# A conditional residual block: the first batch's three small products in plain fp32, and a reordered prologue

## The reference

```
x = x + gamma * layernorm(x + relu(x @ W1 + b1) @ W2 + b2) + beta     (adapter, 256 -> 64 -> 256, language index)
x = x + (x @ Ws^T + bs)                                              (256 -> 256, subject index)
x = x + gated sum of 2 expert nets and 3 shared nets, each relu(x @ wi) @ wo, 256 -> 1024 -> 256
x = x + masked softmax pooling of x                                  (scores from tanh(x @ W + b) @ v)
```

## Time and profile before

| what | value |
|---|---|
| median of 3 runs | 519.26 us (519.24 to 519.38) |
| the profiled execution's own time | 519.18 us |
| its span, first to last instruction | 517.4 us |
| PE busy | 508.7 us (98%) in 2455 instructions |
| DVE, ACT, POOL busy | 325.1 (63%), 262.7 (51%), 232.6 (45%) us |
| mean granted TensorE clock | 0.999 of full speed |
| HBM read, written | 46.76 MB, 2.10 MB |

### The profile page before, as it was taken

How to read it: one execution, slowest core, us unless ns; L and a number is a source line. 1 busy time by engine, 2 the same in 40 slices (tenths; PEclk the granted TensorE clock), 3 DMA queues, 4 the chain that set the end, 5 groups by cost and what they waited for, 6 DMA issues and landing times.

```text
span 517.4 us, 7007 instructions
## 1 busy us (share of the span) xinstructions
PE 508.7 (98%) x2455; PEld 419.4 (81%) x2455; DVE 325.1 (63%) x603; ACT 262.7 (51%) x500; POOL 232.6 (45%) x199
## 2 busy tenths in 40 slices
PE   7899999999999999999999999999999999999997
PEld 4688888888888788888888788888888878888984
DVE  7688223884566864776558675488456686444377
ACT  4655454544447573544446655454444756444233
POOL 2654445445354454444544445444535445655021
PEclk9999999999999999999999999999999999999999
DMA  5634333222224322322223533422222222240002
GB/s 177 191 117 133 103 118 126 82 82 82 82 82 132 103 81 82 122 82 82 81 84 91 147 138 103 121 83 81 82 82 82 81 82 82 94 140 12 0 1 81
DMA packets 44554, 49.30 MB, mean 95 GB/s; under 512 B 7396, under 2 KB 34280, under 8 KB 44520
## 3 DMA queue, kind: packets, MB, share of 16 engines
q1 hardware_dynamic: 42904, 47.03, 28.2%
q10 hardware_dynamic: 1616, 1.84, 1.1%
HBM read 46.76 MB, written 2.10 MB: 94 GB/s over the span
## 4 chain that ended last, share of the span: by engine, by line
PE 96%; DVE 1%; ACT 1%; ACTq 1%; POOL 0%; issue 0%; DVEq 0%
PE ps_hid L789 14%; PE ps_hid L794 14%; PE ps_hid L790 14%; PE ps_net L846 13%; PE ps_net L847 13%; PE ps_net L851 13%; PE ps_net L818 2%; PE ps_side L551 1%; PE ps_side L475 1%; PE ps_side L479 1%; PE ps_side L474 1%; PE ps_side L485 1%; PE ps_side L488 1%; PE ps_side L659 1%; PE ps_side L527 1%; ACTq L1085 0%
## 5 line engine op out<-in xcount | busy, mean ns | idle before, releaser
L1730 DVE SCALAR_TENSOR_TENSOR hid_lo<-ps_hid,hid_hi 128x512 fp32r<-128x512 f32 x160 | 110.5, 690 | 162.7 <-ACT hid_hi L1053 161.7
L1813 POOL TENSOR_TENSOR wi_lo<-raw_wi,wi_hi 128x512 fp32r<-128x512 f32 x78 | 104.2, 1336 | 223.8 <-ACT wo_hi L1032 121.0
L1053 ACT ACTIVATE hid_hi<-ps_hid 128x512 fp32r<-128x512 f32 x160 | 95.6, 598 | 206.0 <-PE ps_hid L794 205.3
L789 PE MATMUL ps_hid<-x2T_hi,wi_lo 128*128 128x512 f32 (+1 forms) x332 | 125.6, 381 | 0.0
L790 PE MATMUL ps_hid<-x2T_hi,wi_hi 128*128 128x512 f32 (+1 forms) x332 | 125.2, 379 | 0.0
L846 PE MATMUL ps_net<-hid_hi,wo_hi 128*128 128x512 f32 x304 | 120.7, 397 | 0.0
L847 PE MATMUL ps_net<-hid_hi,wo_lo 128*128 128x512 f32 x304 | 118.6, 390 | 0.0
L1814 POOL TENSOR_TENSOR wo_lo<-raw_wo,wo_hi 128x512 fp32r<-128x512 f32 x78 | 101.6, 1302 | 0.0
L794 PE MATMUL ps_hid<-x2T_lo,wi_hi 128*128 128x512 f32 (+1 forms) x332 | 99.0, 379 | 0.0
L851 PE MATMUL ps_net<-hid_lo,wo_hi 128*128 128x512 f32 x304 | 93.7, 389 | 0.0
L790 PEld LDWEIGHTS ps_hid<-x2T_hi,wi_hi 128*128 128x128 f32 x332 | 62.4, 188 | 11.9
(11 more groups left out here) (321 smaller groups left out, 506.4 us busy)
## 6 DMA issues: line engine op xcount, KB each, us to landing
raw_wi<-in_L_cond_share_wi_dram SPq DMA_DIRECT2D x23, 512.0 KB, 3.7
raw_wo<-in_L_cond_share_wo_dram SPq DMA_DIRECT2D x23, 512.0 KB, 4.8
raw_wi<-in_L_cond_expert_wi_dram SPq DMA_DIRECT2D x16, 512.0 KB, 3.7
raw_wo<-in_L_cond_expert_wo_dram SPq DMA_DIRECT2D x16, 512.0 KB, 4.8
x_rows<-in_x_dram SPq DMA_DIRECT2D x3, 512.0 KB, 5.8
out_dram<-out_rows SPq DMA_DIRECT2D x5, 256.0 KB, 5.4
gate_w<-in_L_cond_gate_w_dram SPq DMA_DIRECT2D x1, 1024.0 KB, 5.3
subj_w<-in_L_cond_weight_dram SPq DMA_DIRECT2D x3, 256.0 KB, 2.7
```

What stands on the lines that cost most here:

```text
L789: mm(dst, wi_lo[:, w, k, c], x2T_hi[:, k, rows], start=(k == 0), stop=False)
L1053: fn(hid_hi[:, ring(b, q)], ps_hid[:, ring(b, q)], ACT.Relu).then_inc(hid_hi_ready, 1)
L1730: v.scalar_tensor_tensor(out=hid_lo[:, ring(b, q)], in0=ps_hid[:, ring(b, q)], scalar=0.0, in1=f32(hid_hi[:, ring(b, q)]), op0=ALU.max, op ...
L1813: g.tensor_tensor(wi_lo[:, w], raw_wi[:, half % 2, :, c], f32(wi_hi[:, w]), ALU.subtract)
```

## The change

For batch 0 alone, the adapter's two products and the subject product are made in fp32 from unsplit operands. x transposed is kept in x1T (not opT_hi), the bias row b2 becomes row 64 of w2b against a row of ones in hT, and each of the four row tiles has its own bank (`adapted_bank`). x is added on TensorE, by a product with the identity, for tiles 0 and 2, and by VectorE for tiles 1 and 3; statistics are taken tile by tile. ScalarE runs a one-column copy, and with it the table load, right behind the x loads. SP issues b1 ahead of w1 and b2 ahead of w2. ScalarE's order becomes hid0, x_beta(0), x_beta(1) (behind a wait for beta), hid1, norm0, wi of pair 0, subj_wT, wo of pair 0, norm1. TensorE interleaves: hidden(0), tiles 0 and 1, hidden(1), tiles 2 and 3, subj_w, transposes of half 0, 3 fillers, the subject product's first block of half 0, transposes of half 1, its second block, then half 1. The other fillers behind the first 7 go. The step names are adapted, and stage A of the later batches is untouched but for writing hT[0:A].

```diff
-    WARM_XT, WARM_ADAPT, WARM_SUBJ, WARM_NORM, WARM_HALF = 7, 2, 2, 5, 5
+    WARM_XT, WARM_SUBJ = 7, 3
...
-        w2 = sb("w2", [A, D])
-        b2 = sb("b2", [ONE_HI + 1, D])
+        w2b = sb("w2b", [ONE_HI + 1, D])
+        w2, b2 = w2b[0:A], w2b
...
-        hT = sb("hT", [A, S])
+        hT = sb("hT", [A + 1, S])
...
         out_rows = sb("out_rows", [P, R, D])
+        first_subj_wT = out_rows[:, 0:KD]
...
+        def adapted_bank(r):
+            return (ps_net[:, 0], ps_net[:, 1], ps_hid[:, 0], ps_hid[:, 1])[r][:, 0:D]
...
                 with nc.allow_non_contiguous_dma(reason="a few vectors, one element to a partition"):
+                    sp.dma_start(b1[:], L0_b1[la].rearrange("o a -> a o")).then_inc(b1_in, 16)
                     sp.dma_start(w1[:], L0_W1[la].rearrange("o (k p) a -> p (o k) a", p=P)).then_inc(w1_in, 16)
-                    sp.dma_start(b1[:], L0_b1[la].rearrange("o a -> a o")).then_inc(b1_in, 16)
+                    sp.dma_start(b2[ONE_HI:ONE_HI + 1], L0_b2[la]).then_inc(b2_in, 16)
                     sp.dma_start(w2[:], L0_W2[la].rearrange("o a d -> (o a) d")).then_inc(w2_in, 16)
-                    sp.dma_start(b2[ONE_HI:ONE_HI + 1], L0_b2[la]).then_inc(b2_in, 16)
...
                 for h in range(2):
-                    rows = rows_half(h)
-                    pe.wait_ge(p_act.sem, p_act.at(0, f"xhi{h}"))
-                    pe.wait_ge(p_pool.sem, p_pool.at(0, "w1_lo"))
-                    w1_hi, w1_lo = side_by_side(w1_st)
-                    product(ps_hid[0:A, h, 0:HS], [(w1_hi[:, k], w1_lo[:, k], opT_hi[:, k, rows], opT_lo[:, k, rows]) for k in range(KD)],
-                            (p_dve.sem, p_dve.at(0, f"xlo{h}"))).then_inc(p_pe.sem, 1)
-                keep_warm(WARM_ADAPT, warm)
-                for h in range(2):
-                    pe.wait_ge(p_pool.sem, p_pool.at(0, "w2_lo"))
-                    pe.wait_ge(p_dve.sem, p_dve.at(0, f"hlo{h}"))
-                    pe.wait_ge(p_act.sem, p_act.at(0, f"hup{h}"))
-                    adapt_half(ps_net[:, h], h).then_inc(p_pe.sem, 1)
-                keep_warm(WARM_SUBJ, warm)
+                    adapter_hidden(h)
+                    for r in (2 * h, 2 * h + 1):
+                        adapted_rows(r)
                 pe.wait_ge(subj_in, 16)
                 transpose_subj(ps_net[:, 2], True).then_inc(p_pe.sem, 1)
-                keep_warm(WARM_NORM, warm)
-                for h in range(2):
-                    if h == 1:
-                        keep_warm(WARM_HALF, warm)
-                    pe.wait_ge(p_act.sem, p_act.at(0, f"xb{h}"))
-                    pe.wait_ge(p_dve.sem, p_dve.at(0, f"norm{h}"))
-                    pe.wait_ge(p_act.sem, p_act.at(0, f"norm{h}"))
-                    transpose_half(ps_side[:, h], norm, h).then_inc(p_pe.sem, 1)
-                pe.wait_ge(p_dve.sem, p_dve.at(0, "subj_w_lo"))
-                for h in range(2):
-                    x2_half(h)
+                normalised_rows(0)
+                keep_warm(WARM_SUBJ, warm)
+                pe.wait_ge(p_act.sem, p_act.at(0, "subj_wT"))
+                pe.wait_ge(p_dve.sem, p_dve.at(0, "x1T0"))
+                x2_part(0, 0)
+                normalised_rows(1)
+                x2_part(0, 1).then_inc(p_pe.sem, 1)
+                pe.wait_ge(p_dve.sem, p_dve.at(0, "x1T1"))
+                x2_part(1, 0)
+                x2_part(1, 1).then_inc(p_pe.sem, 1)
                 for q in range(2):
                     row_product(q, 0)
-            def x2_half(h):
-                rows, bank = rows_half(h), ps_net[:, h]
-                def add(o, lhsT, rhs, start=False, stop=False):
-                    return mm(bank[:, o * HS:(o + 1) * HS], lhsT, rhs, start=start, stop=stop, skip_group_check=True)
-                pe.wait_ge(p_act.sem, p_act.at(0, f"x1hi{h}"))
-                for o in range(KD):
-                    cols = slice(o * P, (o + 1) * P)
-                    for k in range(KD):
-                        add(o, subj_wT_lo[:, k, cols], opT_hi[:, k, rows], start=(o == 0 and k == 0))
-                        add(o, subj_wT_hi[:, k, cols], opT_hi[:, k, rows])
-                pe.wait_ge(p_dve.sem, p_dve.at(0, f"x1lo{h}"))
-                for o in range(KD):
-                    for k in range(KD):
-                        last = add(o, subj_wT_hi[:, k, o * P:(o + 1) * P], opT_lo[:, k, rows], stop=(k == KD - 1))
+            def adapter_hidden(h):
+                pe.wait_ge(p_act.sem, p_act.at(0, f"xT{h}"))
+                if h == 0:
+                    pe.wait_ge(w1_in, 16)
+                for k in range(KD):
+                    last = mm(ps_hid[0:A, h, 0:HS], w1[:, k], x1T[:, k, rows_half(h)], start=(k == 0), stop=(k == KD - 1))
                 last.then_inc(p_pe.sem, 1)
+            def adapted_rows(r):
+                if r % 2 == 0:
+                    if r == 2:
+                        pe.wait_ge(p_act.sem, p_act.at(0, "hid0"))
+                    mm(adapted_bank(r), ident[:], x_rows[:, r], start=True, stop=False)
+                    pe.wait_ge(p_act.sem, p_act.at(0, f"hid{r // 2}"))
+                    if r == 0:
+                        pe.wait_ge(zeros_ready, 3)
+                        pe.wait_ge(w2_in, 16)
+                        pe.wait_ge(b2_in, 16)
+                mm(adapted_bank(r), hT[:, tile_cols(r)], w2b[:], start=(r % 2 == 1), stop=True).then_inc(p_pe.sem, 1)
+            def normalised_rows(h):
+                pe.wait_ge(p_act.sem, p_act.at(0, f"xb{h}"))
+                pe.wait_ge(p_dve.sem, p_dve.at(0, f"norm{h}"))
+                pe.wait_ge(p_act.sem, p_act.at(0, f"norm{h}"))
+                transpose_half(ps_side[:, h], norm, h).then_inc(p_pe.sem, 1)
+            def x2_part(h, o):
+                for k in range(KD):
+                    last = mm(ps_net[:, h, o * HS:(o + 1) * HS], first_subj_wT[:, k, o * P:(o + 1) * P], x1T[:, k, rows_half(h)],
+                              start=(o == 0 and k == 0), stop=(k == KD - 1), skip_group_check=True)
+                return last
...
                 act.dma_start(x_rows[:, rows], x[0:1, rows_half(h)].rearrange("o (r p) d -> p (o r) d", p=P)).then_inc(x0_in[h], 16)
+            act.wait_ge(zeros_ready, 2)
+            fn(score_col[:, 0:1], ones[:, 0:1], ACT.Copy)
             subj = act.value_load(subj_id.rearrange("(o b) -> o b", o=1)[0:1, 0:1], min_val=0, max_val=L1_weight.shape[0] - 1)
             act.dma_start(subj_w[:], L1_weight[bass.ds(subj, 1)].rearrange("o (k p) d -> p (o k) d", p=P)).then_inc(subj_in, 16)
             for h in range(2):
                 act.wait_ge(p_pe.sem, p_pe.at(0, f"xT{h}"))
-                fn(opT_hi[:, :, rows_half(h)], halves(ps_side[:, h]), ACT.Copy).then_inc(p_act.sem, 1)
+                fn(x1T[:, :, rows_half(h)], halves(ps_side[:, h]), ACT.Copy).then_inc(p_act.sem, 1)
...
             act.dma_start(raw_wo[:, 0], L2_share_wo[net:net + 1, cols].rearrange("o (c p) d -> p (o c) d", p=P)).then_inc(raw_in[0], 16)
-            act.wait_ge(b1_in, 16)
-            for h in range(2):
+            def adapter_hidden(h):
                 act.wait_ge(p_pe.sem, p_pe.at(0, f"hid{h}"))
-                fn(hT[:, rows_half(h)], ps_hid[0:A, h, 0:HS], ACT.Relu, bias=b1[:]).then_inc(p_act.sem, 1)
-            act.wait_ge(p_pool.sem, p_pool.at(0, "w2_hi"))
-            fn(w2_hi[A:P], f32(w2_hi[0:A]), ACT.Copy).then_inc(p_act.sem, 1)
-            for h in range(2):
-                act.wait_ge(p_dve.sem, p_dve.at(0, f"hhi{h}"))
-                fn(hT_both[0:A, rows_half(h)], f32(hT_hi[0:A, rows_half(h)]), ACT.Copy).then_inc(p_act.sem, 1)
-            act.wait_ge(beta_in, 16)
-            for h in range(2):
+                fn(hT[0:A, rows_half(h)], ps_hid[0:A, h, 0:HS], ACT.Relu, bias=b1[:]).then_inc(p_act.sem, 1)
+            def x_beta(h):
                 for k in range(KD):
                     last = fn(xbT[:, k, rows_half(h)], halves(ps_side[:, h])[:, k], ACT.Identity, bias=beta[:, k:k + 1])
                 last.then_inc(p_act.sem, 1)
-            act.wait_ge(p_pe.sem, p_pe.at(0, "subj_wT"))
-            fn(subj_wT_hi[:].rearrange("p k d -> p (k d)"), ps_net[:, 2], ACT.Copy).then_inc(p_act.sem, 1)
             def normalise(h):
                 act.wait_ge(p_pool.sem, p_pool.at(0, f"shift{h}"))
                 r = 2 * h
-                fn(norm[:, r], norm[:, r], ACT.Identity, bias=neg_shift[:, r:r + 1], scale=rstd[:, r:r + 1]).then_inc(p_act.sem, 1)
-            def x1_hi(h):
-                act.wait_ge(p_dve.sem, p_dve.at(0, f"x1T{h}"))
-                fn(opT_hi[:, :, rows_half(h)], x1T[:, :, rows_half(h)], ACT.Copy).then_inc(p_act.sem, 1)
+                fn(norm[:, r], adapted_bank(r), ACT.Identity, bias=neg_shift[:, r:r + 1], scale=rstd[:, r:r + 1]).then_inc(p_act.sem, 1)
+            def first_wi(p):
+                fn(wi_hi[:, p], raw_wi[:, 0, :, 2 * p * P:2 * (p + 1) * P], ACT.Copy)
+            def first_wo(p):
```

(80 more changed lines are left out.)

15 lines of the change are left out of this document (7 added, 8 removed).

## The result

The changed kernel takes **516.31 us** (median of 4 executions, 516.2 to 517.39), the kernel before 519.25 beside it: ratio 0.994 (0.9924 to 0.9955). It is 2.94 us faster; I had forecast 1.65 less, 517.6, in a range of 516.7 to 518.8. The sign was right and the size was not. The execution that was profiled is the slowest of the four, 517.39 us for a span of 515.6, and it is almost the forecast.

What follows compares the result with a forecast made beforehand. Bound: a hand-off chain in the first batch's prologue, before TensorE's unbroken loop products (the train) at 24.55 us. 0.6 us gained before x1T's end plus 1.05 behind it, 1.65 less: 517.6 us by the median, range 516.7 to 518.8.

Steps and rivals of the forecast that it cites:

- Beta keeps its place, its issue time and its traffic: First batch's prologue, SP's loads: beta lands at 9.8 us, and ScalarE's x_beta and hid1 wait for it.
- if it lands in 3.6: Rival on beta's load: ScalarE reaches it at 9.1, gain 2.35, 516.9 us; no chance of its own given.
- w2 too late at 7.7: SP's load order in the prologue: w2 slips by about 0.45 us and lands near 7.7.
- ends in slack: Adapter of batch 0: half 0's win of about 2 us is lost waiting for beta; half 1 keeps 0.7.
- where I had 0.6: Prologue up to the end of x1T of half 1: 17.9 against 18.49, 0.6 us of the gain.
- The 1.05 behind x1T: Subject product: eight fp32 passes without x1's split replace twelve short ones, 1.05 us less; what follows is unchanged.
- The fillers cost nothing: TensorE's prologue: fourteen fillers go and three come; they stood in waits, so they give nothing back.
- the weights were in time: POOL's splits of wi and wo: pairs ready by 18.4 and 21.2, before use, so TensorE's loop products run unbroken.
- the clock rival: TensorE's idle 1.9 us before adapt2 lowers its clock: about 2 to 7 us lost; chance 0.04 brief, 0.06 long.

Runs made afterwards that it cites:

- e7: Kernel before with only the third (subject) product in fp32, the split of x1 gone, its adapter unchanged: 518.7 us, ratio 0.9984.
- e3: Changed kernel with ScalarE making hid1 ahead of the wait for beta and the x_beta operations: 516.7 us, ratio 0.9947.
- e4: Changed kernel without the one-column copy behind the x loads, so the table load precedes the first PSUM copy again: 516.97 us, ratio 0.995.
- e11: Changed kernel with raw loads issued behind the first hT and without the one-column copy at the front: 516.72 us, ratio 0.995.
- e10: Changed kernel with raw loads issued behind the first hT and SP's old order (w1, b1, w2, b2): 516.09 us, ratio 0.9938.
- e1_again: The changed kernel once more, nothing edited, with a common execution profiled: 516.33 us, ratio 0.9944.
- e2: Changed kernel with beta issued behind gamma on SP, some 0.6 us later: 517.75 us, ratio 0.9975.
- e12: Changed kernel with beta issued behind gamma, plus six filler products in TensorE's wait for hid1: 517.55 us, ratio 0.9969.
- e13: Changed kernel with beta issued third on SP and w2 last of the five: 516.77 us, ratio 0.9939.
- e6: Changed kernel with ScalarE's raw loads issued ahead of its copies of transposed x: 518.52 us, ratio 0.9988.
- e9: Changed kernel with hid1 ahead of adapted tiles and beta, tiles 2 and 3 ahead of normalise(0), raw loads behind the second hT: 518.98 us, ratio 1.0002.
- e5: Changed kernel with ScalarE's raw loads issued behind the first hT activation: 516.25 us, ratio 0.9932.
- e8: Changed kernel with hid1 ahead of adapted tiles and beta, and tiles 2 and 3 ahead of normalise(0): 517.26 us, ratio 0.995.
- e14: Changed kernel, hid1 ahead of adapted tiles and beta, tiles 2, 3 before normalise(0), raw loads behind first hT, subj_w's copy before their wait: 517.11 us, ratio 0.9948.

## Why the prediction was wrong, and where it was right

**The step that failed** is this: "Beta keeps its place, its issue time and its traffic: 5.50 + 4.3 = 9.8." Place and issue time it kept (5.44). The 4.3 it did not: raw_wi is issued when TensorE's transposes of x are done, at 5.5 or at 6.05 as the clock rises early or late. By their times, six executions of eight have it behind beta by enough, and beta takes 2.2. In the kernel before nothing would show this: ScalarE reached beta at 10.29, after it had landed either way (4.3 in the trace I had, 2.2 in e7's). I took one landing from one execution as a property of the transfer. The row that should have warned me is raw_wi's issue at the same 5.50 as beta's. I had a rival for it, "if it lands in 3.6", with the range's low end on it at 516.7; it measured 2.2, and the low end had to be 516.2 or lower. The same step had w2 too late at 7.7: with raw_wi behind it by 1.2 us it landed near 7.4, and e3 shows that where it is late as well (8.15) it holds the kernel by itself.

**What followed from it.** "All that the table load, the order of b1 and the dropped splits win for half 0 (about 2 us) thus ends in slack; half 1 keeps 0.7." With beta gone from the chain, half 0's front is the chain again. x1T of half 1 ends at 16.68 against 18.49: 1.81, where I had 0.6. The table load is 0.5 to 0.6 of that (e4, e11); the order of the biases none (e10); the rest, by subtraction, is the adapter without its splits and its wait. Half 0's own gain does not all arrive: adapt2 is done near 11.1 and VectorE takes it at 11.54, since normalise(0) stands in front behind POOL's rstd.

The 1.81 and the 1.05 below make up the 2.86 by which the train starts earlier in e1_again.

**Right, by the rows of both executions.** The first copy at 5.07 and 5.24 (forecast 5.0). In the late-beta execution x_beta at 9.75 (9.8), hT of half 1 ending 11.66 (11.8), var_eps half 1 14.32 (14.4), x1T half 1 17.75 (17.9), x2 19.79 (19.9), train 22.76 (22.9). **The 1.05 behind x1T** holds in either: from x1T's end to the train 5.01 in both (22.76 − 17.75 and 21.69 − 16.68) against 6.06 (24.55 − 18.49), and eight passes of x2 in 1.99 (1.94 + 0.05). In TensorE's old order it is 0.6 (e7). The fillers cost nothing, the weights were in time, and the train ran unbroken.

**Missed beside, in the late-beta execution.** w2 landed near 8.2, not 7.7, and the adapter's second product started at 8.43. Half 0's var_eps came at 11.0, not 10.4, hidden behind half 1; that the numbers of half 1 came out in spite of it is luck. The idle wait of TensorE ahead of adapt2 was with that 0.54, not 1.9, so the clock rival had less to work on than I gave it; in e2, with 1.46, it is real. The Trainium skill, TensorE: Matmul & The Clock Gate, Part 1, makes the throttled state the default that activity releases; e2's 0.50 agrees, and so does e12, where activity put into the wait kept 1.00. The length of the wait alone does not tell: the clock fell behind 1.46 us (e2) and 2.10 us (e13), and did not behind 1.50 us (e6) and 1.95 us (e9), in the profiled execution of each.

## What to carry to other kernels

Before a landing time is carried from one execution into a forecast, look at what was issued on the other queue within a microsecond of it, and at what sets the moment of that issue; if it hangs on a clock or on another engine, there are two landing times, and the sum has to be made with both. Large loads that are wanted late are best issued behind the first work that depends on the small ones (e5 against e6: 516.25 and 518.52 us). And a link that is shortened in front of a wait is in slack only as long as that wait is really there.

## What the hardware showed that I had not expected

- **A small load's time depends on its neighbour on the other queue.** Beta, 1.0 KB in 4-byte pieces: 2.2 us with raw_wi issued 0.6 or 1.8 us later, 4.3 with it 0.07 later, 5.2 with it 0.08 earlier (e8), 4.9 with it 1.0 earlier; but 2.7 in e13 with it 0.8 later. w2, 64 KB: 2.4 and 2.5 with raw_wi 2.4 and 1.2 later, 3.3 with it 0.65 later, 4.3 with it 0.4 earlier; but 2.4 in e12 with it 0.76 later and 2.9 in e10 with it 2.7 later. The order is plain, a rule by the distance is not. The Trainium skill, DMA: Bandwidth & Descriptors, Issuing engines are not separate DMA queues, says that transfers of ScalarE and SyncE run on the same 16 DMA engines and interleave; these runs agree. Beside that they show that a load issued 0.07 to 0.65 us later holds up the one ahead of it; by what way is not shown.
- **TensorE's clock rose at different moments under the same seven fillers**: the eight transposes behind them took 1.05 to 1.92 us, and the record of the upper level begins between 4.16 (e9) and 7.18 us (e4). The first filler starts at 1.18 or 1.19 and the first transpose at 4.14 in all traces of the changed kernel and its variants.
- **Once fallen, the clock stayed down through busy work**: at 0.50 for 3.41 us in e2 and in e13, with TensorE busy for all 3.41 of them.
- **POOL's split held a VectorE operation up to its end.** The 1.35 us of normalise(1) in e14 end at 15.89, just after POOL's split (14.47 + 1.27 = 15.74); in e8 1.33 us end at 16.88, POOL's at 16.73. Without a split ahead of it the operation takes 0.41. The Trainium skill, SBUF — State Buffer, Terms, describes the port pair that these two share as an exclusive lock held for a whole instruction, the loser fully blocked. These rows agree with it: POOL's own 1.27 is as long as its other splits, so it gave nothing up.
